# Preparing an attention's first keys, queries and output products ahead of time in a four-layer cross-attention kernel

## The chip, the core and the metric

One core of a Trainium2 chip runs the whole program in one launch. The metric is the device time of that execution in microseconds (us); lower is better. The engines are named as in the profile: PE (TensorE), with PEld for its weight loads; DVE (VectorE); ACT (ScalarE); POOL (GpSimd); SP (SyncE, which issues transfers).

## What is computed

Sixteen sequences of 56 tokens with 256 features pass through four layers. Each attends over the same 1500 context rows of 128 features; a sequence has its own context. Cut from the reference:

```python
x = L0(x, ctx)              # single-head attention, sigmoid gate, rms norm
x = L1(x, ctx, key_mask)    # 16 heads x 64: layernorm, attention, Wo, layernorm, gelu MLP
x = L2(x, ctx, types, pos)  # see below
x = L3(x, ctx, key_mask)    # as L1, other weights

# L1 and L3
q = layernorm(x) @ Wq * scale ; k, v = split(media @ Wkv)
attn = softmax(where(mask, q @ k.T, neg_inf))
x = x + tanh(attn_gate) * ((attn @ v) @ Wo)
x = x + tanh(ff_gate) * (gelu(layernorm(x) @ W1) @ W2)

# L2, after its self-attention
x = x + sdpa(rms(x) @ cq_w, enc @ ck, enc @ cv) @ cdense_w   # 16 heads x 8
mi = rms(x)
x = x + where(vm, (silu(mi@v_gate) * (mi@v_up)) @ v_down,
                  (silu(mi@l_gate) * (mi@l_up)) @ l_down)
```

## The kernel before

The layers follow each other; each engine runs a list of instructions written out by hand, with semaphores between them. Products of PE go round eight PSUM banks: a `Products` object numbers them, product i goes to bank i mod 8, and `bank_free` waits until product i-8 has been emptied. At some places all four compute engines meet in a `join`: each drains, adds one to `s_join`, and waits for the others.

**Layers 1 and 3** (the second and the fourth). Wk is absorbed into the queries, so that keys and values are the raw context. `pe_queries` computes, for each half of the batch and each pair of heads j, one product `q` (L555: three matmuls that stand for one of higher precision, on a high and a low part of both sides) and two `absorbed` products (L848). DVE and ACT empty them in turns (`out_queries`, L589 and L591). Then comes a join (`l1q`, `l3q`), and `pe_cross`: 112 units (16 sequences of seven units of 128 query rows). Unit u needs three chunks of scores (L1013, nine matmuls), which DVE masks and reduces to maxima (L1126), ACT's exponential (L1097), twelve transposes on PE (L1038), two copies out of PSUM into high and low parts (ACT L1087, DVE L1160), and, in groups of two or three units, sums over the keys (L1026). PE's order is scores(s), sums of an older group, transposes(s-1).

PE needs the high and low parts of keys and queries. POOL makes them for every sequence one ahead (L1166, L1168, L1170), and the bfloat16 mask too (L1199). The first sequence's keys and the first group's queries have no work ahead of them: ACT (L1065, L1072) makes their high parts and DVE (L1103) their low parts, both at the start of `act_cross` and `dve_cross`, behind the join.

**Layer 2** ends with the narrow attention `pe_narrow`: 96 slots, and seven more (s = 96 to 102) in which only the last transposes (`fill`, L1773), the last sums (L1786) and the reciprocals (L1794, L1800) are left. DVE ends it with `output(15)` (L1912 to L1918). After the join `l2` come `cd`, the seven products with cdense_w (L1968, one for each tile of 128 tokens), the residual and the sum of squares for each tile on DVE (L574, L565), the root on ACT (L519), the rows scaled by DVE and ACT (L501, L525), 16 transposes (L475), their copies on DVE (L514), and the gate and up products of the MLP (L1998). Half 0 is tiles 0 to 3, half 1 tiles 4 to 6. The MLP's weights are requested by SP behind the same join (L1959).

Of the kernel before, what the change touches and what calls it, by code (L numbers as in the profile page):

```python
# [17 lines left out]
NT = TOKENS // 128  # L18
# [52 lines left out]
class Products:  # L71
# [7 lines left out]
    def take(self, who):  # L79
# [19 lines left out]
def build(nc, io, out):  # L99
    with ExitStack() as ctx:  # L100
# [50 lines left out]
        def parts(name, width):  # L151
# [34 lines left out]
                 for x in (QO_flat[:, 0:4 * KT * QUAD], sbuf("n_p_T", 4 * KT * QUAD, scope=narrow))]  # L186
# [49 lines left out]
        wq_high = {1: [W_r[:, 4096:5120], W_r[:, 5120:6144]], 3: [XN_r[:, 1792:2816], small_r[:, 0:1024]]}  # L236
# [27 lines left out]
        SS = [x.rearrange("p (h k) -> p h k", h=HEADS) for x in SS_flat]  # L264
        rotA = [A[:, i * 512:(i + 1) * 512] for i in range(2)]
# [9 lines left out]
        s_w = {n: sem(f"s_w_{n}") for n in ("l0", "l0b", "l1q", "l1a", "l1o", "l1u", "l1d", "l2q", "l2a", "l2b", "l3q", "l3a", "l3o",  # L275
# [12 lines left out]
        s_fh, s_fl = sem("s_first_high"), sem("s_first_low")  # L288
# [46 lines left out]
        class Norm:  # L335


            def __init__(self, kind, g, bias, masked, place):
                self.kind, self.g, self.bias, self.masked, self.place = kind, g, bias, masked, place
# [15 lines left out]
            def turn(self, h):  # L355
                for m in range(2 if self.masked else 1):
                    for k in range(2):
                        self.parts[h][m, k] = prod.take("act" if self.bias else "dve")
# [5 lines left out]
        def norm(kind, g, bias, masked, place=None):  # L364
            x = Norm(kind, g, bias, masked, place or [XN[:, 0], XN[:, 1]])
            x.plan(0), x.plan(1)
            return x
# [7 lines left out]
        class Gated:  # L375
            def __init__(self, l):
                self.l = l
                self.q_norm = Norm("layer", f"L{l}_ln_q_g", f"L{l}_ln_q_b", False, [XN[:, 0]])
# [10 lines left out]
            def plan(self):  # L389
# [21 lines left out]
                self.ff_norm = norm("layer", f"L{self.l}_ln_ff_g", f"L{self.l}_ln_ff_b", False, [ff_rows])  # L411
# [30 lines left out]
        cd_prod = [prod.take("dve") for _ in range(NT)]  # L442
        post_norm = norm("rms", "L2_ln_post_attn_w", None, True)
        post_norm.turn(0)
        gu_prod, gu_order = {}, []
        for half in range(2):
            for m in range(2):
                for n in range(len(IT)):
                    if (half, m, n) == (0, 0, 2):
                        post_norm.turn(1)  # L450
                        gu_order.append(("turn", 1))
                    gu_order.append(("gu", m, n, half))
                    gu_prod["gate", m, n, half] = prod.take("act")
# [5 lines left out]
        J = {"q0": 1, "l0": 2, "l1q": 3, "l1": 4, "l2q": 5, "l2": 6, "l3q": 7, "l3": 8, "l3ff": 9}  # L459

        def bank(i):
            return psum[i % 8]

        def bank_free(on, i):

            if i >= 8:
                on.wait_ge(*prod.emptied[i - 8])


        def pe_transposes(e, on, n, h):  # L470
            for (m, k), i in n.parts[h].items():
                bank_free(on, i)
                for j, t in enumerate(TILES[h]):
                    on.wait_ge(*n.rows[m][t])
                    x = e.transpose(bank(i)[:, 128 * j:128 * j + 128], n.place[m][:, t, 128 * k:128 * k + 128], ident)  # L475
# [5 lines left out]
        def dve_rows(e, on, n, h):  # L481
# [13 lines left out]
            for t in TILES[h]:  # L495
                if n.kind == "layer":
                    x = e.tensor_scalar(n.place[0][:, t, :], X[:, t, :], mean_var[:, t, 0:1], st[:, 2, t:t + 1],
                                        ALU.subtract, ALU.mult)
                else:
                    a = 4 if n.masked else 2  # L500
                    x = e.tensor_scalar(n.place[0][:, t, :], X[:, t, :], st[:, a, t:t + 1], None, ALU.mult)  # L501
# [19 lines left out]
        def act_masked_rows(e, on, n, h):  # L521
            act_root(e, on, n.var, h)
            on.wait_ge(*n.mask[h][1])
            for t in TILES[h]:
                e.activation(n.place[1][:, t, :], X[:, t, :], ACT.Copy, scale=st[:, 5, t:t + 1]).then_inc(s_row_act, 1)  # L525
# [32 lines left out]
        def dve_stats(e, on, n, t):  # L558
# [5 lines left out]
            else:  # L564
                e.tensor_tensor_reduce(  # L565
                    out=XN[:, 1, t, :], in0=X[:, t, :], in1=X[:, t, :], scale=1.0, scalar=0.0,
# [258 lines left out]
        def pe_queries(e, on, g):  # L825
# [25 lines left out]
            join(e, on, J[f"l{g.l}q"])  # L851

        def out_queries(e, on, g, me):
# [14 lines left out]
            join(e, on, J[f"l{g.l}q"])  # L868
# [7 lines left out]
        class Cross:  # L876
# [54 lines left out]
            def first(self, k):  # L931

                return s_fl, 7 * self.n + k + 1

            def first_high(self, k):
# [1293 lines left out]
```

## Time and profile before

| | |
|---|---|
| three timed runs | 2419.64, 2423.84, 2424.02 us; median 2423.84 |
| the profiled execution's own time | 2411.01 us |
| its span in the trace | 2409.2 us |
| granted PE clock, mean | 0.981 |
| busy | PE 96%, PEld 78%, DVE 65%, ACT 53%, POOL 26% |

All rows are of the one profiled execution. Its time is 1.8 us over its span, and 12.8 us under the median of the timed runs. A row of the timeline has the start, the time to the end of the last instruction that it merges, the engine, the line, and in brackets the idle time before it and what ended it.

### The profile page before, as it was taken

The numbers are of one execution on the slowest core, as the hardware profiler recorded it, in microseconds if no ns is written. First come the engines' busy times: TensorE is split into PE (matmuls) and PEld (weight loads), VectorE is DVE, ScalarE is ACT, GpSimd is POOL, SyncE is SP. The second block draws the span as 40 slices with busy tenths as digits, with TensorE's granted clock in tenths as the row PEclk, the third lists the DMA queues.
The fourth block names the chain that finished last, engine by engine and source line by source line (L and its number), as shares of the span: only waits on it lengthen the run. The fifth ranks groups of instructions, "written<-read, shape, count | busy, mean of one in ns | idle before, by whom it ended". The sixth has DMA issues, their size and how long they took to land.

```text
span 2409.2 us, 41153 instructions
## 1 busy us (share of the span) xinstructions
PE 2312.6 (96%) x16032; PEld 1883.6 (78%) x16032; DVE 1577.1 (65%) x4254; ACT 1279.2 (53%) x2184; POOL 629.1 (26%) x692
## 2 busy tenths in 40 slices
PE   7978999999999999799999999899999999999999
PEld 3857999999999895456666666456799999999988
DVE  3357777777777657577777776313777777777764
ACT  1235555555555533277777777212555555555553
POOL 0024344443433315200000000010444444343330
PEclk8989999999999999899999999899999999999999
DMA  8810111121110110010000000310011212111010
GB/s 266 221 62 20 46 42 52 37 58 35 54 45 27 54 36 21 14 39 27 27 27 27 27 14 1 125 35 1 20 47 41 59 30 59 42 46 46 27 53 16
DMA packets 36131, 115.96 MB, mean 48 GB/s; under 512 B 4618, under 2 KB 18546, under 8 KB 35938
## 3 DMA queue, kind: packets, MB, share of 16 engines
q1 hardware_dynamic: 33474, 101.04, 13.8%
q10 hardware_dynamic: 2464, 12.29, 2.0%
q8 instruction: 128, 2.10, 0.4%
q14 instruction: 65, 0.53, 0.1%
HBM read 112.40 MB, written 0.92 MB: 47 GB/s over the span
## 4 chain that ended last, share of the span: by engine, by line
PE 89%; ACT 5%; DVE 4%; DMA 1%; issue 0%; ACTq 0%; SPq 0%; DVEq 0%
PE bank L1026 20%; PE bank L1013 19%; PE bank L1038 12%; PE bank L1773 7%; PE bank L555 7%; PE bank L1760 3%; PE bank L1998 3%; PE bank L1786 3%; ACT n_scores L1860 3%; PE bank L651 2%; PE bank L2010 2%; PE bank L1742 2%; PE bank L848 1%; PE bank L1746 1%; PE bank L1224 1%; PE bank L1048 1%
## 5 line engine op out<-in xcount | busy, mean ns | idle before, releaser
L1087 ACT CAST p_T_high<-bank 125x512 fp32r<-125x512 f32 x672 | 350.8, 595 | 516.8 <-PE bank L1038 516.8
L1160 DVE TENSOR_TENSOR p_T_low<-bank,p_T_high 125x512 fp32r<-125x512 f32 x672 | 422.6, 684 | 256.7 <-ACT p_T_high L1087 256.5
L1126 DVE CUSTOM_DVE_ANT_0 scores<-bank,mask 128x500 f32<-128x500 f32 x672 | 418.3, 672 | 1.6 <-PE bank L1013 1.6
L1097 ACT ACTIVATE scores<-scores,row_max 128x1500 f32<-128x1500 f32 x224 | 353.4, 1578 | 9.8 <-DVE row_max L1131 9.8
L1026 PE MATMUL bank<-p_T_high,keys_nat_high 125*128 125x256 f32 (+1 forms) x1152 | 346.0, 300 | 1.7 <-ACT inverse L1094 1.7
L1026 PE MATMUL bank<-p_T_high,keys_nat_low 125*128 125x256 f32 (+1 forms) x1152 | 346.3, 301 | 0.0
L1026 PE MATMUL bank<-p_T_low,keys_nat_high 125*128 125x256 f32 (+1 forms) x1152 | 346.2, 300 | 0.0
L1038 PE MATMUL bank<-ident,scores 128*125 128x128 f32 x2688 | 331.7, 273 | 1.5 <-ACT scores L1097 1.5
L1038 PEld LDWEIGHTS bank<-ident,scores 128*125 128x125 f32 x2688 | 319.0, 188 | 4.2 <-ACT scores L1097 4.1
L1893 DVE CUSTOM_DVE_ANT_0 n_scores<-bank,n_zeros 112x500 f32<-112x500 f32 x384 | 237.4, 674 | 91.9 <-PE bank L1760 91.9
L1013 PE MATMUL bank<-keys_T_high,q_stage_high 128*128 128x500 f32 x672 | 282.0, 420 | 11.8 <-DVE q_stage_low L1103 6.9
L1773 PEld LDWEIGHTS bank<-ident,n_scores 112*125 112x125 f32 x1536 | 187.2, 191 | 115.5 <-issue 54.9
L1013 PE MATMUL bank<-keys_T_high,q_stage_low 128*128 128x500 f32 x672 | 262.6, 391 | 0.0
L1013 PE MATMUL bank<-keys_T_low,q_stage_high 128*128 128x500 f32 x672 | 262.1, 390 | 0.0
L1773 PE MATMUL bank<-ident,n_scores 112*125 112x112 f32 x1536 | 218.3, 286 | 10.3 <-ACT q_and_o L1852 5.8
L1026 PEld LDWEIGHTS bank<-p_T_high,keys_nat_high 125*128 125x128 f32 x1152 | 216.7, 188 | 10.2 <-ACT inverse L1094 2.2
L1026 PEld LDWEIGHTS bank<-p_T_low,keys_nat_high 125*128 125x128 f32 x1152 | 217.0, 188 | 8.5
L1026 PEld LDWEIGHTS bank<-p_T_high,keys_nat_low 125*128 125x128 f32 x1152 | 216.7, 188 | 0.0
L1860 ACT ACTIVATE n_scores<-n_scores,n_stats 112x1500 f32<-112x1500 f32 x128 | 197.7, 1546 | 0.4 <-DVE n_stats L1899 0.4
L1166 POOL CAST q_stage_high<-q_and_o 128x256 fp32r<-128x256 f32 (+1 forms) x94 | 41.5, 441 | 427.6 <-PE bank L1013 427.5
L1013 PEld LDWEIGHTS bank<-keys_T_high,q_stage_high 128*128 128x128 f32 x672 | 127.7, 190 | 32.2 <-issue 8.3
L1013 PEld LDWEIGHTS bank<-keys_T_high,q_stage_low 128*128 128x128 f32 x672 | 127.1, 189 | 26.6
(237 smaller groups left out, 3492.6 us busy)
## 6 DMA issues: line engine op xcount, KB each, us to landing
ctx_T<-in_ctxT SPq DMA_DIRECT2D x32, 750.0 KB, 4.2
ctx_nat<-in_ctx SPq DMA_DIRECT2D x32, 672.0 KB
q_and_o<-in_ctxT SPq DMA_DIRECT2D x16, 750.0 KB, 9.7
n_ctx_T<-in_ctxT SPq DMA_DIRECT2D x16, 750.0 KB, 4.2
q_and_o<-in_ctx ACTq DMA_DIRECT2D x16, 672.0 KB
mask_bytes<-in_mask SPq DMA_DIRECT2D x32, 187.5 KB, 5.2
weights<-in_L_W SPq DMA_DIRECT2D x4, 1024.0 KB, 6.2
ctx_nat<-in_ctx SPq DMA_DIRECT2D x32, 78.0 KB
```

Source lines behind the costliest of these rows:

```text
L555: x = e.matmul(out, left[i], right[j], start=start and n == 0, stop=stop and n == 2)
L1013: m = e.matmul(psum[c][:, 0:CHK], QSs[i][g % 2][:, lo:lo + 128], KTs[j][b % 2][:, cols], start=(n == 0), stop=(n == 2))
L1026: m = e.matmul(psum[6 + g % 2][:, cols_g], KNs[i][b % 2][0:KP, cols], PTs[j][g % 2][0:KP, k, cols_g], start=(k == 0 and n == 0), stop=(k = ...
L1038: m = e.transpose(psum[3 + c][0:KP, 128 * k:128 * k + 128], SB[u % 2][:, (4 * c + k) * KP:(4 * c + k + 1) * KP], ident)
L1087: e.copy(PTs[0][g % 2][0:KP, 4 * c:4 * c + 4, lo:lo + 128], psum[3 + c][0:KP, :].rearrange("p (k r) -> p k r", k=4)).then_inc(s_eh, 1)
L1097: e.activation(SB[s % 2], SB[s % 2], ACT.Exp, bias=mx[:, s % 4, 3:4], accum_out=mx[:, s % 4, 4:5]).then_inc(s_ex, 1)
L1126: e.tensor_tensor_reduce(out=SB[u % 2][:, c * CHK:(c + 1) * CHK], in0=psum[c][:, 0:CHK], in1=mb[:, c * CHK:(c + 1) * CHK], scale=1.0, scal ...
L1160: e.tensor_tensor(low, psum[3 + c][0:KP, :].rearrange("p (k r) -> p k r", k=4), high.bitcast(F32), ALU.subtract).then_inc(s_el, 1)
L1760: e.matmul(psum[r][0:PAIR, 0:CHK], n_q[b % 2][rows, PAIR * hh:PAIR * hh + PAIR], CK[b % 2][rows, c * CHK:(c + 1) * CHK], start=True, stop= ...
L1773: m = e.transpose(psum[4 + t % 2][0:KP, PAIR * k:PAIR * k + PAIR], n_unit(quad, r)[0:PAIR, at:at + KP], ident[0:PAIR, 0:PAIR])
L1860: e.activation(unit, unit, ACT.Exp, bias=n_st[0:PAIR, quad % 2, r, 3:4], accum_out=n_st[0:PAIR, quad % 2, r, 4:5]).then_inc(s_n_ex, 1)
L1893: e.tensor_tensor_reduce(out=n_unit(quad, r)[0:PAIR, c * CHK:(c + 1) * CHK], in0=psum[r][0:PAIR, 0:CHK], in1=n_zeros[0:PAIR, :], scale=1.0 ...
```

## The change

1. POOL takes over the first split. ACT's and DVE's instructions of `first_high` and `first_low` are gone. POOL splits the transposed keys of sequence 0 as soon as the second half of the query norm is transposed, writes the mask, splits the first group's queries when their products are emptied, and splits the other keys behind the last `q` product.
2. The joins `l1q`, `l2` and `l3q` are gone. `pe_cross` waits for each bank by itself (`bank_empty`).
3. In the seven last slots of the narrow attention, PE makes `cd` of tiles 0 to 3 (slot 96), the transposes of half 0 (slot 100), and `cd` of tiles 4 and 5 (slot 101); DVE and ACT do residuals, rows and copies of half 0 in between. `cd` of tile 6 stands behind the MLP's second pair of products, and half 1's transposes further behind.
4. The MLP's weights are requested when the sums of sequence 14 are done, and PE waits for gate and up of each expert by themselves. The two buffers of `n_p_T` change places, so that the last sequence doesn't lie where weights land.
5. `Products.take` can be given a bank, since the order is no longer round.

```diff
     def q(g):
-        us = units_of(g)
+        us, b = units_of(g), g // NG
         lo, n = 128 * (us[0] % RT), 128 * len(us)
+        for h in range(lo // S, (lo + n - 1) // S + 1):
+            on.wait_ge(*prod.emptied[gated.absorbed[h // 2, b // HALF, h % 2]])
...
+    for i in gated.q_norm.parts[1].values():
+        on.wait_ge(*prod.made[i])
+    for c in range(CH):
+        keysT(0, c)
     mask(0)
+    q(0)
+    on.wait_ge(*prod.made[gated.q[7, 1]])
+    for c in range(CH):
+        keys(0, c)
     for s in range(U):
...
 def pe_narrow
+        if s == SLOTS:
+            for r, t in enumerate(TILES[0]):
+                on.wait_ge(*n_maximum(SLOTS - 1, r))
+                pe_cd(e, on, t)
...
+        if s == SLOTS + 4:
+            pe_transposes(e, on, post_norm, 0)
+        if s == SLOTS + 5:
+            n_fills(on, QUADS - 1, 11)
+            for t in TILES[1][:-1]:
+                pe_cd(e, on, t)
...
 def act_narrow
+        if s == SLOTS + 3:
+            act_masked_rows(e, on, post_norm, 0)
...
 def dve_narrow
+    late_residuals = [TILES[0][0:2], TILES[0][2:3], TILES[0][3:4], (), (), (), ()]
...
+        if s >= SLOTS and late_residuals[s - SLOTS]:
+            on.wait_ge(*n_filled(n_last_in(9) // 4, 3 * (n_last_in(9) % 4) + 2))
+            dve_residual(e, on, cd_prod, None, post_norm, late_residuals[s - SLOTS])
+        if s == SLOTS + 3:
+            dve_rows(e, on, post_norm, 0)
+        if s == SLOTS + 5:
+            dve_norm_out(e, on, post_norm, 0)
...
 def sp_l2b
-    on.wait_ge(s_join, ENGINES * J["l2"])
+    on.wait_ge(s_n_pv, B - 1)
+    on.wait_ge(*n_filled(n_last_in(9) // 4, 3 * (n_last_in(9) % 4) + 2))
...
 def pe_mlp
-    on.wait_ge(s_w["l2b"], 128)
     for kind, *at in gu_order:
...
+        if kind == "cd":
+            pe_cd(e, on, NT - 1)
+            continue
         m, n, half = at
+        on.wait_ge(s_w[f"l2{'vl'[m]}"], 32)
...
 def act_mlp
+        if kind == "cd":
+            act_masked_rows(e, on, post_norm, 1)
```

POOL at the entry to the attention of layer 1, before the change: two instructions of the gate of layer 0, then the mask, the second group's queries, the mask and keys of sequence 1.

```order
L769 TENSOR_TENSOR area<-area 128x256
L771 TENSOR_TENSOR area<-area,x_nat 128x256
L1199 TENSOR_SCALAR mask<-mask_bytes 128x1500
L1166 CAST q_stage_high<-q_and_o 128x256
L1170 TENSOR_TENSOR q_stage_low<-q_and_o,q_stage_high 128x256
L1199 TENSOR_SCALAR mask<-mask_bytes 128x1500
L1168 TENSOR_SCALAR keys_T_high<-ctx_T 128x500
```

The same place with the change, from the last two pairs of the first split onward (`keys_T` is the transposed context, `keys_nat` the other; two further pairs of `keys_T` stand ahead of the piece).

```order
L1160 TENSOR_SCALAR keys_T_high<-ctx_T 128x500
L1162 TENSOR_TENSOR keys_T_low<-ctx_T,keys_T_high 128x500
L1193 TENSOR_SCALAR mask<-mask_bytes 128x1500
L1158 CAST q_stage_high<-q_and_o 128x256
L1162 TENSOR_TENSOR q_stage_low<-q_and_o,q_stage_high 128x256
L1160 TENSOR_SCALAR keys_nat_high<-ctx_nat 125x512
L1162 TENSOR_TENSOR keys_nat_low<-ctx_nat,keys_nat_high 125x512
L1160 TENSOR_SCALAR keys_nat_high<-ctx_nat 125x512
L1162 TENSOR_TENSOR keys_nat_low<-ctx_nat,keys_nat_high 125x512
L1160 TENSOR_SCALAR keys_nat_high<-ctx_nat 125x512
L1162 TENSOR_TENSOR keys_nat_low<-ctx_nat,keys_nat_high 125x512
L1158 CAST q_stage_high<-q_and_o 128x256
```

Six splits of keys and one of queries now stand ahead of the second group's queries (the last row), three of them behind the last `q` product.

PE in the last slots of the narrow attention, before the change, from the transposes of slots 97 to 99 to the MLP.

```order
L1773 MATMUL bank<-ident,n_scores 125x112 x48
L1786 MATMUL bank<-n_p_T,n_values 32x224 x16
L1794 MATMUL bank<-ident,n_recip 8x112
L1786 MATMUL bank<-n_p_T,n_values 32x224 x16
L1800 MATMUL bank<-n_recip_T,pick 128x56 x2
L1786 MATMUL bank<-n_p_T,n_values 32x224 x16
L1968 MATMUL bank<-value_weights,q_and_o 128x256 x7
L475 MATMUL bank<-ident,x_normed 128x128 x16
L1998 MATMUL bank<-x_T,weights 128x448 x8
L475 MATMUL bank<-ident,x_normed 128x128 x12
```

And with the change (`cd` is L1997 now; four of them stand ahead of slot 96's transposes, before this piece).

```order
L1779 MATMUL bank<-ident,n_scores 125x112 x48
L1792 MATMUL bank<-q_and_o,n_values 32x224 x16
L1800 MATMUL bank<-ident,n_recip 8x112
L496 MATMUL bank<-ident,area 128x128 x16
L1792 MATMUL bank<-q_and_o,n_values 32x224 x16
L1806 MATMUL bank<-n_recip_T,pick 128x56 x2
L1997 MATMUL bank<-value_weights,q_and_o 128x256 x2
L1792 MATMUL bank<-q_and_o,n_values 32x224 x16
L2018 MATMUL bank<-x_T,weights 128x448 x8
L1997 MATMUL bank<-value_weights,q_and_o 128x256
L2018 MATMUL bank<-x_T,weights 128x448 x12
L496 MATMUL bank<-ident,x_normed 128x128 x12
```

The seven `cd` and the 16 transposes have left the place between the last sums and the MLP.

## Rows read from the trace of the kernel before

**Rows 1.** The page's part 4: shares of the chain that ended last.

```profile
PE 89%; ACT 5%; DVE 4%; DMA 1%; issue 0%; ACTq 0%; SPq 0%; DVEq 0%
```

**Rows 2.** Busy time by stretch; behind POOL's: granted clock, DMA share, GB/s.

```profile
300.00:1080.00 780.00, 754.84 (x5286) 649.17 (x5284) 549.48 (x1436) 410.20 (x714) 272.14 (x292) 0.99 0.13 40
...
1500.00:1514.00 14.00, 13.13 (x85) 9.66 (x88) 1.96 (x4) 5.39 (x10) 0.00 (x0) 0.52 0.01 1
1525.00:1538.00 13.00, 8.52 (x23) 5.54 (x24) 7.52 (x25) 5.05 (x10) 0.00 (x0) 0.50 1.06 347
```

**Rows 3.** Timeline, entry to the attention of layer 1.

```profile
184.72 1.50 PE L555 MATMUL bank<-x_T_r,weights_r 128*128 128x448 f32 x6
...
186.14 1.77 PE L848 MATMUL bank<-area,weights 64*128 64x448 f32 x8
...
191.36 0.47 PE L1013 MATMUL bank<-keys_T_high,q_stage_high 128*128 128x500 f32 x1 [3.44 <-DVE q_stage_low L1103]
...
191.89 0.39 PE L1013 MATMUL bank<-keys_T_high,q_stage_low 128*128 128x500 f32 x1
...
196.30 0.67 DVE L1126 CUSTOM_DVE_ANT_0 scores<-bank,mask 128x500 f32<-128x500 f32 x1
...
198.40 1.55 ACT L1097 ACTIVATE scores<-scores,row_max 128x1500 f32<-128x1500 f32 x1 [4.90 <-DVE row_max L1131]
...
200.57 1.47 PE L1038 MATMUL bank<-ident,scores 128*125 128x128 f32 x12
...
201.80 0.47 PE L1013 MATMUL bank<-keys_T_high,q_stage_high 128*128 128x500 f32 x1
...
202.64 1.57 ACT L1097 ACTIVATE scores<-scores,row_max 128x1500 f32<-128x1500 f32 x1
...
204.35 1.58 PE L1038 MATMUL bank<-ident,scores 128*125 128x128 f32 x12 [0.27 <-ACT scores L1097]
```

**Rows 4.** Timeline, entry to the attention of layer 3.

```profile
1689.97 1.77 PE L848 MATMUL bank<-area,weights 64*128 64x448 f32 x8
...
1705.94 0.47 PE L1013 MATMUL bank<-keys_T_high,q_stage_high 128*128 128x500 f32 x1
```

**Rows 5.** POOL's groups of instructions by form, the whole span.

```profile
L1170 POOL TENSOR_TENSOR keys_nat_low<-ctx_nat,keys_nat_high 125x512 fp32r<-125x512 f32 x90 | 116.0, 1289 | 7.5
...
L1168 POOL TENSOR_SCALAR keys_nat_high<-ctx_nat 125x512 fp32r<-125x512 f32 x90 | 55.8, 620 | 188.4 <-DMA ctx_nat<-in_ctx 188.4
...
L1170 POOL TENSOR_TENSOR q_stage_low<-q_and_o,q_stage_high 128x256 fp32r<-128x256 f32 x62 | 45.8, 739 | 5.0
...
L1166 POOL CAST q_stage_high<-q_and_o 128x256 fp32r<-128x256 f32 x62 | 25.3, 408 | 259.4 <-PE bank L1013 259.3
```

**Rows 6.** Timeline of POOL while DVE had two SBUF operands.

```profile
194.91 0.92 POOL L1168 TENSOR_SCALAR keys_T_high<-ctx_T 128x500 fp32r<-128x500 f32 x1
...
195.92 1.55 POOL L1170 TENSOR_TENSOR keys_T_low<-ctx_T,keys_T_high 128x500 fp32r<-128x500 f32 x1
```

**Rows 7.** Timeline of PE, layer 2's last slots and the MLP's start.

```profile
1496.47 1.13 PE L1773 MATMUL bank<-ident,n_scores 112*125 112x112 f32 x8
...
1499.31 9.11 PE L1773 MATMUL bank<-ident,n_scores 112*125 112x112 f32 x40 [1.72 <-ACT n_p_T L1852]
...
1515.59 1.72 PE L1786 MATMUL bank<-n_p_T,n_values 125*32 125x224 f32 x32
...
1518.68 3.29 PE L1968 MATMUL bank<-value_weights,q_and_o 128*128 128x256 f32 x14 [1.38 <-DVEq L317]
...
1525.52 3.73 PE L475 MATMUL bank<-ident,x_normed 128*128 128x128 f32 x16 [3.54 <-DVE x_normed L501]
...
1533.22 8.69 PE L1998 MATMUL bank<-x_T,weights 128*128 128x448 f32 x16 [3.97 <-DVE x_T L514]
...
1541.74 1.47 PE L475 MATMUL bank<-ident,x_normed 128*128 128x128 f32 x12
1543.05 17.41 PE L1998 MATMUL bank<-x_T,weights 128*128 128x448 f32 x45
```

More of the change, by code:

```diff
@@ L77, in __init__, with take @@
         self.who, self.made, self.emptied = [], [], []
-    def take(self, who):
+        self.banks, self.ahead, self.last = [], [], {}
+    def take(self, who, at=None):
+        if at is None:
+            at = (self.banks[-1] + 1) % 8 if self.banks else 0
+        self.ahead.append(self.last.get(at))
+        self.last[at] = len(self.who)
+        self.banks.append(at)
         self.who.append(who)
@@ L362, in plan_cut, with rows_of, norm @@
                     self.cut[h][k] = high_low(cut_steps)
-        def norm(kind, g, bias, masked, place=None):
-            x = Norm(kind, g, bias, masked, place or [XN[:, 0], XN[:, 1]])
+        def rows_of(x):
+            return [x[:, t, :] for t in range(NT)]
+        def norm(kind, g, bias, masked, place=None, squares=None):
+            x = Norm(kind, g, bias, masked, place or [rows_of(XN[:, 0]), rows_of(XN[:, 1])],
+                     squares or rows_of(XN[:, 1]))
             x.plan(0), x.plan(1)
@@ L452, in build @@
                     gu_order.append(("gu", m, n, half))
-                    gu_prod["gate", m, n, half] = prod.take("act")
+                    at = 0 if (half, m, n) == (0, 0, 0) else None
+                    gu_prod["gate", m, n, half] = prod.take("act", at)
                     gu_prod["up", m, n, half] = prod.take("dve")
@@ L458, in build @@
         g3.plan()
-        J = {"q0": 1, "l0": 2, "l1q": 3, "l1": 4, "l2q": 5, "l2": 6, "l3q": 7, "l3": 8, "l3ff": 9}
+        J = {"q0": 1, "l0": 2, "l1": 3, "l2q": 4, "l3": 5, "l3ff": 6}
         def bank(i):
-            return psum[i % 8]
+            return psum[prod.banks[i]]
         def bank_free(on, i):
-            if i >= 8:
-                on.wait_ge(*prod.emptied[i - 8])
+            if prod.ahead[i] is not None:
+                on.wait_ge(*prod.emptied[prod.ahead[i]])
         def pe_transposes(e, on, n, h):
@@ L1000, in sp_cross, with pe_cross, bank_empty @@
                     mask(b), keysT(b), keys(b)
-        def pe_cross(e, on, x):
+        def pe_cross(e, on, x, gated):
+            last = gated.absorbed[7, 1, 1]
+            product_in = {prod.banks[i]: i for i in range(last - 7, last + 1)}
+            def bank_empty(k):
+                on.wait_ge(*prod.emptied[product_in[k]])
             def scores(u):
@@ L1706, in n_unit, with n_last_in @@
             return n_scores[(4 * quad + r) % 10]
+        def n_last_in(k):
+            return max(u for u in range(4 * QUADS) if u % 10 == k)
         def n_fills_of(s):
```

145 lines of the change are left out of this document (58 added, 87 removed).

## The prediction

> **What bounds the kernel now.** I read the chain that ended last first: PE has 89% of it, ACT 5%, DVE 4% [rows 1]. Then the busy time by stretch: in a dense piece of layer 1's attention PE is busy 754.84 of 780 us at a clock of 0.99 [rows 2]. There only fewer or faster PE instructions would help, and the change has neither. So I looked for places where PE stands still although the program has work, and went through the timeline at the three joins that go.
>
> Entry to layer 1's attention: PE's last product of the queries ends at 186.14 + 1.77 = 187.91. Then PE waits 3.44 us for the low part of the first queries, makes unit 0's scores from 191.36, and unit 2's scores start only at 201.80 [rows 3]. Reader: the first maximum is at 196.30, because DVE splits keys until then. Layer 3 repeats it: 1691.74 to 1705.94, 14.2 us [rows 4].
>
> End of layer 2's attention: the last sums end at 1515.59 + 1.72 = 1517.31, the MLP's first product starts at 1533.22. These 15.9 us hold only 3.29 us of cd products and 3.73 us of transposes; the rest is a chain through DVE and ACT and back. The clock was 0.52 in 1500 to 1514 and 0.50 in 1525 to 1538 [rows 2, 7].
>
> **Entry to layer 1.** Gone from the path: ACT's and DVE's splits. New chain from 187.91, with the old durations:
> - Unit 0's first chunk takes 191.89 + 0.39 - 191.36 = 0.92 us [rows 3]: ready at 188.83, and DVE's maximum starts at about 188.9. No bank is waited for, since banks 0 to 2 hold products three pairs old.
> - From the first maximum to the exponential were 198.40 - 196.30 = 2.10 us. PE delivers a chunk about every 0.7 us, little slower than DVE takes them, so I add 0.1: exponential at 191.1.
> - From there to the transposes: 204.35 - 202.64 = 1.71 (unit 1; unit 0's own 2.17 holds scores at the low clock): 192.8. Unit 1's scores end at about 191.9 and don't delay this.
> - Transposes to unit 2's scores: 201.80 - 200.57 = 1.23: 194.1 [rows 3].
>
> Before 201.80, now 194.1: **7.7 us** less. After that the cadence of the first units is a chain of transposes, copies, exponential that doesn't change, and later PE is full; neither gives anything back.
>
> What has to be ready: POOL. The first three key pairs, the mask and the first queries start when the second norm half is transposed, with eleven q products still to come, each 1.50 us and its absorbed ones [rows 3], more than 16 us. They take 3 x 2.5 + 1.5 even by POOL's slow rows [rows 6], and a mask; the query products hide them. Behind the last q product (184.72 + 1.50 = 186.22 [rows 3]) come three pairs of 0.62 + 1.29, with gaps 5.9 us, and the second group's queries, 0.41 + 0.74 and a gap, 1.2 us [rows 5]: ready at 193.4, 0.7 before unit 2 asks. This is the tight place. By the slow rows, 0.92 and 1.55, a pair takes 2.5 us and the queries 1.5 [rows 6]: ready at 195.3 to 195.6, up to 1.5 us late. I take nothing, since DVE's maxima and evacuations there have PSUM on one side; the slow rows fell where DVE had two SBUF operands. Behind the second group's queries wait the next mask and keys, needed a unit or more later.
>
> The earlier splits fall beside DVE's four splits of the normed queries. If each of those waited for one POOL instruction, DVE would be 2 x (0.62 + 1.29) = 3.8 us later [rows 5], and PE behind it by at most as much. I take nothing again: banks of several products lie between.
>
> **Entry to layer 3.** 1689.97 + 1.77 = 1691.74; unit 2's scores would start 194.1 - 187.91 = 6.2 later, at 1697.9, instead of 1705.94 [rows 4]: **8.0 us**. It has 0.3 more because the clock was low there.
>
> **End of layer 2.** The gap of 15.9 us goes. What it held comes back elsewhere on PE's path:
> - Four cd in slot 96: eight of 14 records of 3.29 us [rows 7], 1.9 us. They are not free. They stand ahead of slot 96's transposes, ACT waits for these, and PE's idle 1.72 us comes behind them and only moves. DVE's two residuals fit into the time in which it waits.
> - Sixteen transposes in slot 100: 3.73 at the low clock; 16/12 of 1.47 = 2.0 at the full one [rows 7]. The clock fell when PE had waited 1.72 us and came back at about 1514, which moves by 1.9; the transposes would start at about 1514.4, so part is slow: 2.8.
> - Two cd in slot 101: 0.9, one inside the MLP: 0.5.
> - Slot 101's sums come after the clock's return: 0.7 less.
> - The MLP's first 16 records took 8.69 us; at 17.41/45 = 0.387 each they take 6.2 [rows 7]. PE comes there without a pause, so the clock should be full: 2.5 less.
>
> 15.9 - 1.9 - 2.8 - 0.9 - 0.5 + 0.7 + 2.5 = **13.0 us**. Hidden, I think: half 0's chain (root, rows) in slot 100's sums. PE waited 3.54 us for it before [rows 7], with a table load in it that now lies ahead, and two sums groups take some 3 us at the low clock; I take it as just hidden, and what it is late by shows in full. The copies to x_T lie in slot 101, beside sums. The weights are requested before slot 97's transposes, which stood at 1499.31, some 20 us ahead of the MLP. Half 1's root brings two more ACT table loads into the MLP; the silu behind them frees a bank that is asked for three pairs of products later, 3 x 8 x 0.387 = 9.3 us [rows 7].
>
> Bounds: if the clock stays low from 1502 through the MLP's start, 15.9 - 1.9 - 3.7 - 0.9 - 0.5 = 8.9. If it never falls, the 48 transposes before (40 of them 9.11 us) go at 1.13 for 8, 3.5 us less, and the sums 2.3 less: 15.9 - 1.9 - 2.0 - 0.9 - 0.5 + 2.5 + 5.8 = 18.9 [rows 7].
>
> **Sum.** 7.7 + 8.0 + 13.0 = 28.7 us. The profiled execution's 2411.01 would become 2382.3. The timed median is 12.8 us above it; the same step gives 2423.84 - 28.7 = **2395.1 us**.
>
> **Rivals.**
> 1. POOL and DVE block each other. For it: 0.92 where the mean is 0.62, 1.55 where it is 1.29 [rows 5, 6]. Then the second group's queries are 1.5 us late and the queries' products up to 3.8, at both entries: 28.7 - 10.6 = 18.1, 2405.7 us at worst, and about 2401 if half. Against it: POOL ran beside DVE all through the attention, and its means are those of the undisturbed rows. The Trainium skill ("SBUF — State Buffer", Who interferes with whom) says that DVE and GpSimd lock a shared pair of ports for a whole instruction and the later one blocks fully, when DVE has two SBUF inputs. By that rule this rival has its cause; the worst case above, 18.1, is what it would leave of the 28.7. In this trace POOL's instructions beside DVE's stretched by 0.3 us only, so the trace agrees with a wait, not with its full length.
> 2. The clock stays low in layer 2's tail and the MLP's start: 8.9 there, 24.6 in all, 2399.2 us. For it: the tail keeps its idle 1.72 us, and low stretches lasted 13 us or more [rows 2, 7].
> 3. The entries give nothing: another chain holds the first units, POOL's or the loads', and only layer 2's 13.0 remain: 2410.8 us. Against it: POOL is 272 of 780 us busy in the attention [rows 2].
> 4. The change doesn't do what it says: PE waits in slot 100 for rows or in the MLP for weights as long as it did before, and the entries are as in 3: within 4.8 us of before.
> 5. Slower: with fewer pauses the chip holds PE's clock low for a piece of the attention. A stretch of 75 us at half clock costs about 37 us where PE is full; beyond 57 us of it the 28.7 are used up, and at 75 it would be 2432 us. Against it: the clock is 0.99 in the densest stretch [rows 2].
>
> **How the numbers follow.** Chances: forecast 0.72 (own range 2391 to 2399), rival 1 0.12, rival 2 0.08, rival 3 0.03, rival 4 0.02, rival 5 0.03. The unknown costs alone reach from 34.6 us (8.0 + 7.7 + 18.9) to 14.0 (2.4 + 2.7 + 8.9), 2389 to 2410. At the fast end I add that the profiled execution lay 12.8 us below the timed ones, so that runs differ by more than the three shown; at the slow end I leave out rivals 3 to 5 and the worst of 1. Range 2384 to 2403. What a measurement of this kernel can tell from no change is about 0.2%, 4.8 us. Faster by more: 0.72 + 0.12 + 0.08 + 0.03 = 0.95, with a little of rival 4 0.96; same 0.01; slower 0.03.
>
> **What would show it.** Entry right: exponential of unit 0 3.2 us behind the last absorbed product, unit 2's scores 6.2 behind it, no wait of PE for q_stage. Wrong: PE waits there for POOL's q_stage_low or a bank. Layer 2 right: sums of slot 102 followed at once by the gate product, 0.375 to 0.39 us a record; wrong: PE waits at the transposes for row scaling, or at the gate for weights or x_T; a clock of 0.5 beyond 1520 means rival 2. Longer DVE instructions at the second norm half mean rival 1. The prediction fails too if unit 1's transposes come later than 3.8 us behind unit 0's (204.35 - 200.57 [rows 3]), or if the dense stretch changes its length.

## The result, and the profile after

| | us |
|---|---|
| before, median of four timed runs | 2422.53 (2419.64 to 2424.02) |
| changed, median of four timed runs | 2389.70 (2386.29 to 2393.81) |
| ratio, 95% interval | 0.9871 (0.9857 to 0.9885) |
| span of the profiled execution of each | 2409.2 and 2392.0 |

Timed, the change takes away 31 to 33 us (31.2 by the ratio, 32.8 by the medians); 28.7 were predicted. One further execution of the kernel before, in the set of e1 to e3, took 3081.45 us at a mean granted clock of 0.70 and is in no ratio here. The two profiled executions differ by 17.2 us only; where the rest went is read below. Lines have moved: L1013, L1038, L1097, L1126 are L1032, L1059, L1105, L1118 now; L555 and L848 are L576 and L869; L1773, L1786, L1998 are L1779, L1792, L2018.

The page's part 4 and the busy time by stretch of the changed kernel (to [rows 1, 2]; behind POOL's busy time the granted clock):

```profile
PE 90%; ACT 5%; DVE 3%; DMA 2%; issue 0%; ACTq 0%; SPq 0%; DVEq 0%
```

```profile
300.00:1080.00 780.00, 755.37 (x5183) 647.64 (x5185) 543.31 (x1417) 404.50 (x704) 272.61 (x292) 0.98 0.13 40
1506.00:1520.00 14.00, 10.46 (x102) 7.73 (x100) 8.31 (x29) 11.68 (x21) 0.00 (x0) 1.00 0.86 302
1526.00:1539.00 13.00, 13.00 (x51) 6.76 (x43) 6.47 (x22) 6.15 (x10) 0.00 (x0) 1.00 0.84 251
```

The attention is as dense as before. At layer 2's end and in the MLP's start the granted clock is 1.00, the full level of 2.4 GHz, where it was about 0.5, the level of 1.2 GHz [rows 2].

Timeline of the changed kernel at the entry to layer 1's attention (to [rows 3]):

```profile
193.34 1.77 PE L869 MATMUL bank<-area,weights 64*128 64x448 f32 x8
...
195.04 0.49 PE L1032 MATMUL bank<-keys_T_high,q_stage_high 128*128 128x500 f32 x1
...
195.75 1.28 ACT L1105 ACT_TABLE_LOAD   x1
...
196.13 0.68 DVE L1118 CUSTOM_DVE_ANT_0 scores<-bank,mask 128x500 f32<-128x500 f32 x1 [0.36 <-PE bank L1032]
...
198.12 1.30 POOL L1162 TENSOR_TENSOR keys_nat_low<-ctx_nat,keys_nat_high 125x512 fp32r<-125x512 f32 x1
...
198.29 1.55 ACT L1105 ACTIVATE scores<-scores,row_max 128x1500 f32<-128x1500 f32 x1 [1.26 <-DVE row_max L1123]
...
199.84 0.73 POOL L1162 TENSOR_TENSOR q_stage_low<-q_and_o,q_stage_high 128x256 fp32r<-128x256 f32 x1
199.98 1.58 PE L1059 MATMUL bank<-ident,scores 128*125 128x128 f32 x12 [0.60 <-ACT scores L1105]
...
201.31 0.47 PE L1032 MATMUL bank<-keys_T_high,q_stage_high 128*128 128x500 f32 x1
```

The last absorbed product ends at 193.34 + 1.77 = 195.11 and unit 0's scores follow with no wait. The exponential starts 3.2 us behind it, unit 2's scores 201.31 - 195.11 = 6.2 us; before it was 13.9 [rows 3]. GpSimd has the second group's queries at 199.84 + 0.73 = 200.57, 0.7 us before they are taken. Layer 3, the last absorbed product and the start of unit 2's scores (to [rows 4]):

```profile
1681.47 1.77 PE L869 MATMUL bank<-area,weights 64*128 64x448 f32 x8
...
1689.62 0.47 PE L1032 MATMUL bank<-keys_T_high,q_stage_high 128*128 128x500 f32 x1
```

1689.62 - 1683.24 = 6.4 us, before 14.2. Both gains still stand at the eighth unit, whose transposes start 41.0 and 41.2 us behind the last absorbed product, before 48.7 and 49.0.

Layer 2's end. I measure it from the reciprocals' rows of sequence 14, which both kernels have. Timeline of PE, the kernel before:

```profile
1491.99 0.65 PE L1800 MATMUL bank<-n_recip_T,pick 8*128 8x56 f32 x4
```

And the changed kernel (to [rows 7]):

```profile
1500.76 0.65 PE L1806 MATMUL bank<-n_recip_T,pick 8*128 8x56 f32 x4
1501.34 1.99 PE L1997 MATMUL bank<-value_weights,q_and_o 128*128 128x256 f32 x8
...
1509.81 2.59 PE L1779 MATMUL bank<-ident,n_scores 112*125 112x112 f32 x16 [1.72 <-ACT q_and_o L1868]
...
1519.51 2.31 PE L496 MATMUL bank<-ident,area 128*128 128x128 f32 x16
...
1523.98 1.13 PE L1997 MATMUL bank<-value_weights,q_and_o 128*128 128x256 f32 x4
1525.04 1.72 PE L1792 MATMUL bank<-q_and_o,n_values 125*32 125x224 f32 x32
1526.69 6.28 PE L2018 MATMUL bank<-x_T,weights 128*128 128x448 f32 x16
...
1532.81 0.59 PE L1997 MATMUL bank<-value_weights,q_and_o 128*128 128x256 f32 x2
1533.24 9.18 PE L2018 MATMUL bank<-x_T,weights 128*128 128x448 f32 x24
```

The MLP's first product follows the last sums directly. PE waits 1.72 us for ACT as before, but behind it the transposes go at 0.16 us a record instead of 0.23 [rows 7]. The stretch ends where all seven cd and the MLP's first 16 records are done: before at 1541.74, where half 1's transposes start [rows 7], after at 1533.24, the MLP's 17th record. That is 49.75 us before, 32.48 after, 17.3 less. (Half 1's transposes lie behind this point in both kernels.)

So the three places give 7.7 + 7.8 + 17.3 = 32.8 us, and the timed medians differ by 32.8, while these two traces differ by 17.2. The rest lies where the programs are the same: layer 1's last absorbed product ended at 187.91 before and at 195.11 here (7.2 us), and from there to the reciprocals' rows of sequence 14 the changed kernel took 1305.65 us and the one before 1304.08, though the entry is 7.7 us shorter: 9.3 us more, most of it at the start of the narrow attention (below). That can be noise of two executions or a side effect of the change; four traces (e2, e4, e9, e10) ask which.

### The profile page after: what moved, and what is told of

Its sections match the earlier page's. It is cut to its first block, busy times and chain, and to the rows that moved or that the text cites. A ratio compares the mean times of both kernels' runs of the same rounds, so it can differ in the third digit from the quotient of the medians.

```text
span 2392.0 us, 41182 instructions
## 1 busy us (share of the span) xinstructions
PE 2313.8 (97%) x16032; PEld 1883.7 (79%) x16032; DVE 1567.3 (66%) x4240; ACT 1274.8 (53%) x2172; POOL 654.0 (27%) x720
## 3 DMA queue, kind: packets, MB, share of 16 engines
q1 hardware_dynamic: 33474, 101.04, 13.9%
## 4 chain that ended last, share of the span: by engine, by line
PE 90%; ACT 5%; DVE 3%; DMA 2%; issue 0%; ACTq 0%; SPq 0%; DVEq 0%
PE bank L1045 20%; PE bank L1032 19%; PE bank L1059 12%; PE bank L1779 7%; PE bank L576 7%; PE bank L1766 3%; PE bank L2018 3%; PE bank L1792 3%; ACT n_scores L1876 3%; PE bank L672 2%; PE bank L1748 2%; PE bank L2031 2%; PE bank L869 1%; PE bank L1752 1%; PE bank L1226 1%; PE bank L1071 1%
## 5 line engine op out<-in xcount | busy, mean ns | idle before, releaser
L1118 DVE CUSTOM_DVE_ANT_0 scores<-bank,mask 128x500 f32<-128x500 f32 x672 | 418.5, 673 | 0.8 <-PE bank L1032 0.8
L1105 ACT ACTIVATE scores<-scores,row_max 128x1500 f32<-128x1500 f32 x224 | 353.4, 1578 | 2.7 <-DVE row_max L1123 2.7
L1059 PE MATMUL bank<-ident,scores 128*125 128x128 f32 x2688 | 331.1, 273 | 2.7 <-ACT scores L1105 2.7
L1059 PEld LDWEIGHTS bank<-ident,scores 128*125 128x125 f32 x2688 | 318.2, 187 | 5.7 <-ACT scores L1105 5.7
L1032 PE MATMUL bank<-keys_T_high,q_stage_high 128*128 128x500 f32 x672 | 280.1, 417 | 0.0
L1779 PEld LDWEIGHTS bank<-ident,n_scores 112*125 112x125 f32 x1536 | 187.0, 190 | 117.7 <-issue 55.7
L1032 PE MATMUL bank<-keys_T_high,q_stage_low 128*128 128x500 f32 x672 | 261.2, 389 | 0.0
L1032 PE MATMUL bank<-keys_T_low,q_stage_high 128*128 128x500 f32 x672 | 260.7, 388 | 0.0
L1779 PE MATMUL bank<-ident,n_scores 112*125 112x112 f32 x1536 | 218.4, 286 | 10.6 <-ACT q_and_o L1868 5.3
L1032 PEld LDWEIGHTS bank<-keys_T_high,q_stage_low 128*128 128x128 f32 x672 | 126.2, 188 | 26.3
L1032 PEld LDWEIGHTS bank<-keys_T_high,q_stage_high 128*128 128x128 f32 x672 | 126.9, 189 | 19.0 <-issue 1.6
```

What stands on the lines that cost most here:

```text
L1032: m = e.matmul(psum[c][:, 0:CHK], QSs[i][g % 2][:, lo:lo + 128], KTs[j][b % 2][:, cols], start=(n == 0), stop=(n == 2))
L1059: m = e.transpose(psum[3 + c][0:KP, 128 * k:128 * k + 128], SB[u % 2][:, (4 * c + k) * KP:(4 * c + k + 1) * KP], ident)
L1105: e.activation(SB[s % 2], SB[s % 2], ACT.Exp, bias=mx[:, s % 4, 3:4], accum_out=mx[:, s % 4, 4:5]).then_inc(s_ex, 1)
L1118: e.tensor_tensor_reduce(out=SB[u % 2][:, c * CHK:(c + 1) * CHK], in0=psum[c][:, 0:CHK], in1=mb[:, c * CHK:(c + 1) * CHK], scale=1.0, scal ...
L1779: m = e.transpose(psum[4 + t % 2][0:KP, PAIR * k:PAIR * k + PAIR], n_unit(quad, r)[0:PAIR, at:at + KP], ident[0:PAIR, 0:PAIR])
```

## The experiments

**My theory**: three independent pieces (two entries, layer 2's end), of which the entries' gain is GpSimd's split, and the last is larger than predicted since PE's clock stays full. **Rivals**: the tail's clock was luck and 13.0 is the usual gain; the joins, not the split, cost the time; the change slows layer 0 and the narrow attention's start. Every ratio below is to the kernel before, timed in the same set, with its 95% interval.

**e1: the entries alone.** The kernel before, with part 1 of the change and without the joins `l1q` and `l3q`; cut from it:

```diff
-            join(e, on, J[f"l{g.l}q"])
...
-            def first_high(k, dst, src, sem, value):
...
-            def first_low(k, dst, src, high):
...
+            for c in range(CH):
+                keysT(0, c)
+            mask(0)
+            q(0)
```

> The kernel before with part 1 of the change and the joins l1q and l3q gone; layer 2's end and its join as before. My theory, three pieces that add up: 7.7 + 7.8 = 15.5 us less than before (ratio 0.9936); unit 2's scores 6.2 to 6.4 us behind the last absorbed product at both entries; the end of layer 2 keeps its idle 1.72 us, its low clock until the sums, and 15.9 us between last sums and MLP. Rival A, that the entries give nothing lasting and the time comes from elsewhere: less than 5 us. Rival B, that the change itself made layer 0 and the start of the narrow attention slower (7.2 and 8.8 us in the profile after): those stretches are long here too, and the gain is near zero or negative in the span.

Measured: ratio 0.9927 (0.9905 to 0.9950), 17.7 us; unit 2's scores 6.2 and 6.4 us behind the last absorbed product, as expected (15.5 us lie inside the interval). Layer 2's end as before: 49.5 us, clock low behind the pause.

**e2: the tail alone.** The changed kernel with the joins `l1q` and `l3q`, `first_high` and `first_low` back.

> The changed kernel with the first split, the joins l1q and l3q and their waits as before; only parts 2 (join l2) to 5 of the change remain. My theory: the clock stays full at layer 2's end because of what the new order does there, and the tail gives about 17 us (ratio 0.993). Rival, as I predicted it blind: the clock falls to 0.5 behind the idle 1.72 us as it did before, the tail gives 13.0 us (8.9 if it stays low to the MLP), and the profile after was one of the executions in which it didn't. The granted clock in the profile between slot 97 and the MLP tells: 1.00 against 0.5. Entries: 13.9 and 14.2 us from last absorbed product to unit 2's scores, as before.

Measured: 0.9934 (0.9911 to 0.9957), 16.0 us. Entries 13.1 and 13.5 us. The two alone make 33.7 us, 0.9861 as a product, against 0.9871 together: within the intervals, the pieces add up. In its trace the clock did fall. Windows and timeline of PE:

```profile
1512.00:1526.00 14.00, 11.57 (x64) 10.18 (x66) 6.51 (x25) 9.77 (x18) 0.00 (x0) 0.59 0.88 302
```

```profile
1505.46 0.65 PE L1826 MATMUL bank<-n_recip_T,pick 8*128 8x56 f32 x4
...
1514.51 9.60 PE L1799 MATMUL bank<-ident,n_scores 112*125 112x112 f32 x40 [1.72 <-ACT q_and_o L1888]
...
1528.12 1.91 PE L497 MATMUL bank<-ident,area 128*128 128x128 f32 x16
...
1541.45 3.92 PE L2038 MATMUL bank<-x_T,weights 128*128 128x448 f32 x10
```

From the reciprocals' rows to the MLP's 17th record: 1541.45 - 1505.46 = 36.0 us, 13.8 less than before. That is the case I had predicted as the likeliest (13.0). From the reciprocals' rows to the MLP the two kernels give PE the same list, and here the clock fell, while it stayed full in the changed kernel. e2 has one trace; whether one and the same kernel does both at this place is not shown.

**e3 and e11: cd into the idle time.** Both are one kernel, the changed one with this edit:

```diff
-                if s == SLOTS:
-                    for r, t in enumerate(TILES[0]):
-                        on.wait_ge(*n_maximum(SLOTS - 1, r))
-                        pe_cd(e, on, t)
                 for half in range(2):
+                    if (s, half) == (SLOTS + 1, 1):
+                        for r, t in enumerate(TILES[0]):
+                            on.wait_ge(*n_maximum(SLOTS - 1, r))
+                            pe_cd(e, on, t)
...
-            late_residuals = [TILES[0][0:2], TILES[0][2:3], TILES[0][3:4], (), (), (), ()]
+            late_residuals = [(), TILES[0][0:2], TILES[0][2:4], (), (), (), ()]
```

> The changed kernel with its four cd products moved from ahead of slot 96's transposes into slot 97, between the two halves of its transposes, where PE stood idle for 1.72 us waiting for ACT; DVE's residuals of half 0 one slot later. My theory: they cost 1.99 us of PE's path in slot 96 and will cost 0.3 in the idle time, so 1.7 us less than the changed kernel, about 33 us less than before (ratio 0.9864 against 0.9871). Rival: ACT or DVE is what holds slots 97 to 100 (the residuals come a slot later and half 0's root with them), PE then waits in slot 100 for the rows: no gain or up to 1 us lost.

> e3_cd_in_idle again, timed beside the changed kernel. My theory: 1.7 us less than it by PE's path, and up to 3 us less on the mean if the clock never falls where there is no pause (the two traces without the pause kept it full). Rival: equal within what the timing can tell; the clock falls here too in some executions, behind the 0.77 us that PE still waits in slot 98.

Measured: 0.9858 (0.9836 to 0.9881), and 0.9847 (0.9827 to 0.9867) beside the changed kernel's 0.9866 in e10. Timeline of PE in e3:

```profile
1499.79 0.65 PE L1806 MATMUL bank<-n_recip_T,pick 8*128 8x56 f32 x4
...
1505.22 1.91 PE L1997 MATMUL bank<-value_weights,q_and_o 128*128 128x256 f32 x8
1507.11 2.59 PE L1779 MATMUL bank<-ident,n_scores 112*125 112x112 f32 x16
...
1530.53 9.18 PE L2018 MATMUL bank<-x_T,weights 128*128 128x448 f32 x24
```

The wait of 1.72 us is filled. The stretch is 1530.53 - 1499.79 = 30.74 us instead of 32.48, 1.74 less, as expected, in both traces. Both medians lie 2 us under those of the changed kernel (2387.76 against 2389.70 in another set, 2386.28 against 2388.37 in the same), but the intervals overlap: the trace shows the gain, the timing can't tell it. By its medians it is the fastest version of the study.

**e4, e9, e10: unedited kernels again.**

> The changed kernel once more, unedited, for its trace. If the 7.2 us in layer 0 (a context load that came late) and the 8.8 us around the start of the narrow attention (clock 0.5 to 0.7 for some microseconds) belong to the change, they stand here again; if they are of that one execution, they are gone or elsewhere. The same for the clock at layer 2's end: at 1.00 again if the new order keeps it, at 0.5 in some executions if it is chance.

> The kernel before once more, unedited, for a second trace of it. My theory: its first profiled execution was an uncommonly quick one in stretches that the change doesn't touch. The last absorbed product of layer 1 ended at 187.91 there and at 192 to 196.4 in every other kernel's trace, two of which have the same code up to that point; I expect 192 to 196 here, and a span near 2420. Rival: the changed layouts or numbers of semaphores slow the later kernels' first layer; then it is 188 again. The end of layer 2: idle 1.72 us, and behind it the clock falls or stays.

> The changed kernel, timed beside e11 on the same chip. Ratio to before 0.987; its trace is one more sample of the clock at layer 2's end (it fell in two of the six traces so far that have this end and its idle 1.72 us).

Measured: e4 one time, 2389.21 us; e9 one time, 2423.59; e10 0.9866 (0.9843 to 0.9889). Layer 1's last absorbed product ended at 195.78 in e4, 192.23 in e9, 184.93 in e10, and at 193.31 in e2, whose program is that of before up to there: a spread of 11 us, and the changed kernel has both ends of it. For the narrow attention's start, the stretch 1000 to 1060 of before, e9, e4 and e10, in this order (clock behind POOL's):

```profile
1000.00:1060.00 60.00, 52.39 (x307) 31.42 (x308) 40.21 (x116) 27.96 (x46) 2.11 (x4) 0.95 0.12 39
...
1000.00:1060.00 60.00, 48.79 (x230) 27.60 (x230) 36.22 (x99) 20.39 (x32) 2.11 (x4) 0.80 0.12 39
...
1000.00:1060.00 60.00, 52.52 (x277) 31.31 (x277) 36.88 (x107) 24.86 (x40) 2.11 (x4) 0.86 0.12 39
...
1000.00:1060.00 60.00, 53.76 (x288) 30.76 (x286) 39.13 (x113) 30.08 (x49) 2.11 (x4) 0.89 0.12 39
```

The kernel before has 0.95 in one trace and 0.80 in the other; the changed kernel has 0.80 in its first trace, 0.86 and 0.89 here, and 0.95 in e5. The first profiled execution of the kernel before was quick in both places beside its second, and the side effect falls as a rival. e9's span less e4's is 34.4 us. Layer 2's end in e9 has the low clock again: 0.54 in 1512 to 1526, 49.8 us.

**e5: the joins without the old split.**

```diff
+            join(e, on, J[f"l{g.l}q"])
...
             q(0)
+            e.drain().then_inc(s_join, 1)
```

The first line stands behind the queries of PE, ACT and DVE; the other is GpSimd's, which adds its one and doesn't wait.

> The changed kernel with the joins l1q and l3q put back behind the last queries; GpSimd only adds its one to s_join when it has split the first queries and doesn't wait, so that its work stays where it is. My theory: the entries' gain is nearly all from the split. With the join, unit 0's scores start about 1.0 us behind the last absorbed product instead of at once (0.6 us of emptying, then a semaphore's way), unit 2's scores 7.2 to 7.6 us behind it instead of 6.2 to 6.4: the joins are worth 1.0 to 1.2 us each, the split 6.5. Rival: the joins are the larger part (the waits of four engines for each other), unit 2's scores stand 9 us or more behind.

Measured: 8.4 and 9.6 us to unit 2's scores instead of 6.2 and 6.4; in time 0.9876 (0.9858 to 0.9895), not to be told from the changed kernel's. Timeline of the entry to layer 1:

```profile
192.52 1.77 PE L869 MATMUL bank<-area,weights 64*128 64x448 f32 x8
195.05 0.49 PE L1034 MATMUL bank<-keys_T_high,q_stage_high 128*128 128x500 f32 x1 [0.76 <-DVEq L325]
...
198.35 1.28 ACT L1107 ACT_TABLE_LOAD   x1 [3.44 <-DVE row_max L1125]
...
199.65 1.55 ACT L1107 ACTIVATE scores<-scores,row_max 128x1500 f32<-128x1500 f32 x1
```

Neither number was right. The join itself costs 0.8 us, little less than I gave it; but in this version ACT's table load for the exponential stands behind the wait for unit 0's maximum at both entries, 1.28 us in the middle of the chain, where the changed kernel has it at 195.75, while ACT has nothing else. The kernel before had the join too, but its load ran ahead of that wait, at 192.21, behind ACT's first splits: only the kernel with the join and without those splits has the load there. At layer 3 the clock fell besides: behind the same idle 1.94 us of PE the twelve transposes took 1.58 us at layer 1 (granted clock 1.00) and 2.92 at layer 3 (0.51). So the split is worth 4 to 5.5 of the 7 to 8 us of an entry, and the join with what came with it here 2 to 3.

**e6: the slack of the second group's queries.**

```diff
+                if s == 0:
+                    mask(1), keysT(1, 0), q(1)
+                    continue
```

> The changed kernel with GpSimd's split of the second group's queries moved behind the mask and the first keys of sequence 1 (1.44 and 1.86 us, some 3.4 with gaps). In the trace after, these queries were ready 0.7 us before unit 2's scores took them. My theory: the slack is 0.7 us and no more, unit 2's scores come 2.7 us later, 8.9 to 9.1 us behind the last absorbed product at both entries, 4 to 5.4 us in the whole time. Rival: another chain (copies, maxima) leaves slack behind it and takes the delay up again within the first units, so that the third transposes stand where they stood.

```profile
204.88 0.49 PE L1032 MATMUL bank<-keys_T_high,q_stage_high 128*128 128x500 f32 x1 [2.60 <-POOL q_stage_low L1162]
```

Measured: 9.0 us at both entries, 0.9901 (0.9877 to 0.9924). At unit 2's scores the delay is 2.8 us at layer 1 and 2.7 at layer 3. The eighth unit's transposes stand 43.3 us behind the last absorbed product instead of 41.0, and at layer 3 44.8 instead of 41.2: of the delay 2.3 us are left at layer 1, and 3.7 are there at layer 3, 6.0 in all, where I expected 4 to 5.4. The rival, that another chain takes it up, falls. The slack was the 0.7 us that I read.

**e7: the weights late.**

```diff
-            on.wait_ge(s_n_pv, B - 1)
-            on.wait_ge(*n_filled(n_last_in(9) // 4, 3 * (n_last_in(9) % 4) + 2))
+            on.wait_ge(s_n_pv, B)
```

> The changed kernel with the MLP's weights requested only when the last sums are done (about where the join let them go before), instead of 20 us ahead. In the trace after, they landed 4.1 and 5.5 us (first expert) and 6.7 and 8.0 us (second) behind their issue. My theory: the early request hides all of it; PE waits at the gate product for the first expert's weights, 5.5 to 6.5 us between the end of the last sums and the MLP where there was nothing, and the time is about 6 us longer. Rival: the products of the first expert start in part, the transfers are faster when nothing else moves, and it costs under 3 us. In passing: does the clock at the MLP fall behind that idle time?

```profile
1519.88 1.72 PE L1792 MATMUL bank<-q_and_o,n_values 125*32 125x224 f32 x32
1527.70 8.16 PE L2017 MATMUL bank<-x_T,weights 128*128 128x448 f32 x16 [6.10 <-DMA weights<-in_L_v_up]
```

Measured: PE waits 6.10 us, as expected, and the 16 records behind it take 8.16 instead of 6.28 us, in part at the low clock (0.77 in the mean). 0.9906 (0.9887 to 0.9924), by the ratios some 8.5 us more than the changed kernel, where I expected 6. The clock fell besides before that, behind the second pause, ahead of any wait for the weights: 19.8 us from the first pause's end to the last sums' end instead of 16.95. Without part 4 of the change the gap comes back in part.

**e8: unit 0's scores ahead of the last four absorbed products**, on e3. DVE and ACT empty these four behind unit 0's maxima and ahead of its exponential, and GpSimd splits the second group's queries ahead of the other keys. Cut from it:

```diff
+            scores(0)
+            pe_products(e, on, gated, gated.order[-4:])
             for s in range(U + 4):
-                if s < U:
+                if 0 < s < U:
                     scores(s)
```

> A version meant to be faster, on e3_cd_in_idle: unit 0's scores stand ahead of the last four absorbed products, whose outputs DVE and ACT empty behind unit 0's maxima and ahead of its exponential, and GpSimd splits the second group's queries before the other keys. My theory: the entry is bound by the chain scores, maxima, exponential, transposes of unit 0, which starts 1.77 us earlier, of which PE's own work leaves about 0.9: unit 2's scores 5.3 us behind the end of the last absorbed product's former place, in all some 2 us for both entries, ratio about 0.985 to the kernel before (e3: 0.9858). Rival: PE has no idle time left there that counts, since transposes, copies and exponential of units 1 and 2 set the pace; then it equals e3_cd_in_idle.

```profile
197.42 0.55 ACT L611 ACTIVATE q_and_o<-bank 128x448 f32<-128x448 f32 x1 [0.21 <-PE bank L873]
...
197.98 1.28 ACT L1112 ACT_TABLE_LOAD   x1
...
199.28 1.55 ACT L1112 ACTIVATE scores<-scores,row_max 128x1500 f32<-128x1500 f32 x1
```

Measured: 0.9869 (0.9848 to 0.9890), and in the trace unit 2's scores come 0.8 us (layer 1) and 0.6 us (layer 3) later than in e3, counted from the last `q` product. My theory falls. The rival, no gain, is what the timing can't exclude; the trace has the entry longer. The maximum is ready at 196.87, but ACT first empties the moved products (to 197.97) and loads its table: it was ACT's place in the chain that I had not priced.

**e12: the first splits behind DVE's cuts.**

```diff
-            for i in gated.q_norm.parts[1].values():
-                on.wait_ge(*prod.made[i])
+            for steps in gated.q_norm.cut[1].values():
+                on.wait_ge(*steps[1])
```

> The changed kernel with GpSimd's first splits of keys held back until DVE has cut the second half of the query norm, instead of beside it. In the trace after, DVE's two subtractions of the cut took 1.51 and 1.50 us beside them, 0.56 before. My theory: the two engines hold each other up there, and DVE's rows return to 0.56 while GpSimd's first keys go at 0.62 and 1.25; the time doesn't change, because PE's products go on with banks in hand (they kept their 2.37 us for each pair). Rival: the rows are long for another reason (placement of the buffers), and stay at 1.5.

Timeline of the changed kernel, and (last two rows) of e12:

```profile
169.76 1.25 POOL L1162 TENSOR_TENSOR keys_T_low<-ctx_T,keys_T_high 128x500 fp32r<-128x500 f32 x1
169.92 1.51 DVE L558 TENSOR_TENSOR x_T_r<-x_T,x_T_r 128x384 fp32r<-128x384 f32 x1
...
170.98 0.92 POOL L1160 TENSOR_SCALAR keys_T_high<-ctx_T 128x500 fp32r<-128x500 f32 x1
```

```profile
171.71 0.56 DVE L558 TENSOR_TENSOR x_T_r<-x_T,x_T_r 128x384 fp32r<-128x384 f32 x1
172.41 0.61 POOL L1160 TENSOR_SCALAR keys_T_high<-ctx_T 128x500 fp32r<-128x500 f32 x1 [27.65 <-DVE x_T_r L558]
```

Measured: DVE's subtractions return to 0.56 us, GpSimd's first step to 0.61. One time, 2388.68 us, and 6.2 and 6.4 us at the entries. All four instructions of DVE's cut took 4.3 us in the changed kernel (169.33 to 173.65), 1.8 here and before. The two engines do hold each other up, and it costs nothing here.

## Why the prediction was right, and where it was off

- **The number.** 2389.70 us lie inside the whole range (2384 to 2403) and 1.3 us below the forecast's own (2391 to 2399). The case that came, the clock full through layer 2's end, had a price in the prediction, 18.9, but no chance of its own. Only with that bound do the unknown costs reach down to 2389.
- **Entries (7.7 and 8.0 predicted, 7.7 and 7.8 in the traces).** Each step held: exponential 3.2 us behind the last absorbed product, no bank waited for, unit 2's scores at 6.2, the second group's queries 0.7 us ahead (e6 shows that there is no more). Against the other traces with the old entries (13.1 us in e2 and e9 at layer 1, 13.5 and 14.2 at layer 3) the gain is 6.9 to 7.7 and 7.1 to 7.8. By the letter one sign of being wrong came true, without weight: unit 1's transposes start 3.89 us behind unit 0's, not 3.78. The step missed a condition that it stands on: with the first splits gone from ACT, its table load is off the chain only as long as the join is gone too (e5).
- **Rival 1 (GpSimd and DVE block each other).** Its cause was there, stronger than my rows of before showed: 1.51 us instead of 0.56. DVE's subtraction starts at 169.92 and ends 0.42 behind the end of GpSimd's; had it only begun there, it would end 0.56 behind. That is close to full blocking. By the rule of the Trainium skill that I cited ("SBUF — State Buffer", Who interferes with whom) this is what had to be expected, and the trace now agrees with it to 0.14 us. DVE's cut became 2.5 us longer, where I had 3.8 at most. My argument that it would cost no time held for the reason given: from the first q product behind the norm's second half to the last one PE took 23.24 us, as before, and e12 without contention has the same entries.
- **End of layer 2 (13.0 predicted, 17.3 measured).** The mis-sized term is the clock in slots 98 to 102. I had it fall behind the idle 1.72 us as in [rows 7]; it stayed full, and from the pause's end to the last sums' end PE took 1526.76 - 1509.81 = 16.95 us with two cd and 16 transposes in it, 13.65 without them (2.24 and 1.06 of path), against 18.0 before: 4.35 less, where I had 0.7. The sixteen transposes took 2.24 instead of 2.8, the four cd 1.8 instead of 1.9. The MLP's 2.5 measured 2.4, and PE came to it without a pause. This is near the bound of 18.9 that I gave for a clock that never falls; e2 shows the forecast case, 13.8. What the timed gain has beyond 28.7 is thus owed to the clock, which I had on the wrong side, and it is the bound, not the forecast, that had this case.
- **Half 0's chain "just hidden".** Nearly: the 16 transposes took 2.31 us at the full clock, but 1.91 in e2 and e7, where PE came to them later. They were held up for 0.4 us; ACT ended its last rows at 1520.77, 1.26 us behind the first transposes' start, in e2 0.65 ahead of it.
- **What decides the clock there stays open.** With the old end it was low behind the pause in all three traces (before, e1, e9). With the new end it stayed full in six (the changed kernel, e4, e5, e6, e10, e12) and fell in two: in e2 behind the 1.72 us, in e7 behind a second pause of 0.76. With cd in the pause it stayed full in three of three (e3, e8, e11). No kernel shows both: the kernel before fell in two traces of two, the changed one stayed full in three of three, e3's in two of two. The new order may favour the full clock, by the cd records, or it may be chance; no set of traces here is large enough to tell.
- **Sum.** With the entries' mean over the traces (13.4 and 14.0 before, so 7.2 + 7.6) and the tail's (32.5 six times, 36.0 once: 33.0, against 49.7; 16.7) the gain is 31.5 us; the ratio 0.9871 gives 31.2.
- **Rivals 2 to 5** did not occur in the changed kernel's traces; the nearest to rival 2 are e2, with the low clock up to half 0's transposes, and e7. The offset of the profiled execution (12.8 us) was of that one execution: e9 ran at 2423.59.

## What to carry to other kernels

When a serial place is found, price each engine's own list in it, table loads included: the same load was free ahead of a wait and cost 1.28 us behind it (e5) or behind moved work (e8). Products that must run anyway belong into the next known idle time of their engine, not at the first point at which their data is there (e3). And before two single traces are compared, compare stretches in which the programs are equal: here these alone differed by more than 15 us.

## What the runs showed of the chip

- GpSimd's and DVE's subtractions between SBUF operands, side by side: DVE 1.51 instead of 0.56 us, GpSimd's next step 0.92 instead of 0.61. Over the whole span of the kernel before, with DVE busy for 65% of it, GpSimd's means are 0.62 and 1.29 [rows 5].
- PE's granted clock behind the same idle time differs from one execution of a kernel to the next. At the entry to layer 1, behind 3.44 us, the kernel before had 1.00 for unit 0's scores and 0.57 for unit 1's (191.3 to 194.0, 197.0 to 200.6); in e9, the same kernel, it was 0.51 and 1.00 (195.6 to 198.5, 200.9 to 203.0). The entry took 13.9 and 13.1 us.
- At layer 2's end the 40 transposes behind the pause take 9.1 to 9.6 us where the clock fell at once and, with two short waits between them, 7.2 where it stayed full. Such a fall made the stretch 3.5 us longer in e2.
- The end of layer 1's last absorbed product, with the same program up to the norm, varied between 184.9 and 196.4 us over the traces, and so does the whole time by some us.
